# A decoder on one core: how the first layer's preparation waits, and what TensorE does meanwhile

## The reference

```python
mixed_qkv = hidden_states @ W_qkv                  # 128 -> 2048 channels
z = (hidden_states @ W_z).reshape(b_, t_, HV, DV)
beta = jax.nn.sigmoid(hidden_states @ W_b)
g = -jnp.exp(A_log) * jax.nn.softplus(hidden_states @ W_a + dt_bias)
mixed_qkv = _causal_conv_silu(mixed_qkv, conv_w)   # 4 taps along the tokens, then silu
q, k, v = jnp.split(mixed_qkv, [K_DIM, 2 * K_DIM], axis=-1)
...
q = _l2norm(q) * DK ** (-0.5)                      # _l2norm: x * rsqrt(sum(x * x) + EPS) per head
k = _l2norm(k)
```

## Time and profile before

| | us |
|---|---|
| median of 3 runs (lowest, highest) | 4723.59 (4719.43, 4734.4) |
| the profiled execution's own time | 4747.6 |
| its span, first to last instruction | 4745.9 |
| mean granted TensorE clock | 0.921 |

### The profile page before, as it was taken

The page is one execution under the profiler, slowest core; times in us unless marked ns, Lnnn a source line. Parts: engine busy times, 40 slices in busy tenths (PEclk is TensorE's granted clock), DMA queues, the critical chain, the costliest instruction groups (busy, mean ns, idle before and its releaser), DMA issues. The chain is left out here.

```text
span 4745.9 us, 96485 instructions
## 1 busy us (share of the span) xinstructions
PE 4029.2 (85%) x38268; PEld 2457.0 (52%) x38268; DVE 2463.7 (52%) x6106; ACT 1541.4 (32%) x3476; POOL 822.1 (17%) x1452
## 2 busy tenths in 40 slices
PE   6998787898799878789879977878887997787888
PEld 3883343465488334346548833434654883343465
DVE  4674534454567453445456744335545674434553
ACT  3452222341345222234134422223413442222431
POOL 1430000130153000013014300011301430001120
PEclk7998999999799899999979998999997998899999
DMA  2001000000000100000000010000000001000000
GB/s 80 3 3 43 15 18 18 22 36 25 25 3 3 51 7 18 18 22 36 25 25 3 3 57 1 18 18 22 35 25 25 3 8 52 8 11 18 23 35 27
DMA packets 11005, 105.56 MB, mean 22 GB/s; under 512 B 1148, under 2 KB 5552, under 8 KB 6192
## 3 DMA queue, kind: packets, MB, share of 16 engines
q1 hardware_dynamic: 10544, 99.21, 5.4%
HBM read 98.16 MB, written 1.05 MB: 21 GB/s over the span
## 5 line engine op out<-in xcount | busy, mean ns | idle before, releaser
L88 PE MATMUL psum<-ident_bf 128*128 128x512 bf16 x1784 | 515.5, 428 | 204.2 <-DVE l_attn_peak L770 66.6
L88 PEld LDWEIGHTS psum<-ident_bf 128*128 128x128 bf16 x1784 | 178.2, 108 | 465.3 <-issue 172.9
L3044 DVE TENSOR_TENSOR l_attn_xx<-l_attn_xx,psum 128x256 f32<-128x256 f32 x512 | 204.6, 419 | 207.4 <-PE psum L2649 195.6
L2811 ACT ACTIVATE l_attn_ax<-psum 128x128 f32<-128x128 f32 (+1 forms) x768 | 184.9, 279 | 366.1 <-PE psum L2630 251.4
L399 DVE TENSOR_TENSOR l_ffn_hidden<-l_ffn_silu,psum 128x512 f32<-128x512 f32 (+2 forms) x184 | 126.3, 686 | 325.3 <-ACT l_ffn_silu L340 325.1
L94 PEld LDWEIGHTS psum<-streamed_weights,l_ffn_hidden 128*128 128x128 f32 (+2 forms) x1728 | 226.0, 192 | 113.3 <-issue 99.8
L340 ACT ACTIVATE l_ffn_silu<-psum 128x512 f32<-128x512 f32 (+2 forms) x216 | 128.9, 597 | 475.9 <-PE psum L310 475.9
L2645 PE MATMUL psum<-l_attn_ax,l_attn_xx 64*64 64x64 f32 x5120 | 265.0, 222 | 0.0
L2649 PE MATMUL psum<-l_attn_xx,l_attn_ax 64*64 64x64 f32 x5120 | 258.2, 219 | 0.0
L770 DVE TENSOR_REDUCE l_attn_peak<-psum 128x4 f32<-128x2048 f32 (+3 forms) x128 | 185.9, 1487 | 126.2 <-PE psum L688 125.4
L2938 POOL TENSOR_TENSOR l_attn_part<-l_attn_ab,streamed_weights 128x128 f32<-128x128 f32 x640 | 243.3, 413 | 20.3 <-PE psum L2630 20.3
(11 more groups left out here) (522 smaller groups left out, 8141.6 us busy)
## 6 DMA issues: line engine op xcount, KB each, us to landing
streamed_weights<-pack_l_ffn SPq DMA_DIRECT2D x4, 5412.0 KB, 15.4
streamed_weights<-pack_l_ffn SPq DMA_DIRECT2D x4, 3972.0 KB, 13.3
streamed_weights<-pack_l_attn SPq DMA_DIRECT2D x5, 2848.5 KB, 9.4
streamed_weights<-pack_l_xattn SPq DMA_DIRECT2D x4, 2496.0 KB, 8.7
streamed_weights<-pack_l_ffn SPq DMA_DIRECT2D x4, 2192.0 KB, 8.0
streamed_weights<-pack_l_xattn SPq DMA_DIRECT2D x4, 2048.0 KB, 7.4
streamed_weights<-pack_l_ffn SPq DMA_DIRECT2D x4, 1923.0 KB, 8.0
streamed_weights<-pack_l_attn SPq DMA_DIRECT2D x4, 1107.5 KB, 4.9
```

The lines of the kernel that those rows point to most:

```text
L88: pe.matmul(self.bank(bank), self.ident_bf[:, :], self.ident_bf[:, :].unsqueeze(1).to_broadcast([P, NT, P]), start=True, stop=True)
L2811: act.activation(ax[b, p, :, :], m.psum[b, p, 0:P].rearrange("p (i t) -> p i t", i=2), ACT.Copy).then_inc(ax_ready, 1)
L3044: dve.tensor_tensor(both, both, m.psum[:, p, P:384], ALU.subtract).then_inc(x_less, 1)
```

## The change

Six edits, all in the preparation:

- `rsT` has 128 partitions; GpSimd clears it at the start of the block (a new semaphore, `rsT_cleared`), and ScalarE still writes 16 of them. The matrix of `spread` gets zeros in its other 112 rows, and its product runs over 128 rows. The packed array keeps its size.
- TensorE gets 8 identity products ahead of its wait for the roots at n = 11, and 6 ahead of the wait in front of projection 12.
- ScalarE's exp and logarithm go from n = 1 to n = 11, ahead of the copy of the turned roots, and VectorE's three instructions for g from n = 2 to n = 13.

```diff
-        rsT = psb("rsT", [HV, T])
+        rsT = psb("rsT", [P, T])
...
                     if n >= 2:
-                        if n <= NEWTON:
-                            m.warm(pe, 4, 7)
+                        if n <= NEWTON + 2 and n != NEWTON + 1:
+                            m.warm(pe, 4 if n <= NEWTON else 6, 7)
                         pe.wait_ge(conv_ready, n - 1)
...
                     if n == NEWTON + 1:
+                        m.warm(pe, 8, 7)
                         pe.wait_ge(rs_ready, 1)
...
-                    if n == 1:
+                    if n == NEWTON + 1:
                         act.activation(a_exp[:, :], w["a_log"], ACT.Exp)
                         act.activation(g_log[:, :, :], g_log[:, :, :], ACT.Ln).then_inc(logged, 1)
-                    if n == NEWTON + 1:
                         act.wait_ge(rs_turned, 1)
-                        act.activation(rsT[:, :], m.psum[0:HV, 6, :], ACT.Copy).then_inc(rsT_ready, 1)
+                        act.wait_ge(rsT_cleared, 1)
+                        act.activation(rsT[0:HV, :], m.psum[0:HV, 6, :], ACT.Copy).then_inc(rsT_ready, 1)
...
+                pool.memset(rsT[:, :], 0.0).then_inc(rsT_cleared, 1)
                 for i in range(2 * F):
...
-                    if n == 2:
+                    if n == NEWTON + 3:
                         dve.wait_ge(logged, 1)
...
-            ... ("spread", const["spread16"])]
+            ... ("spread", np.concatenate([const["spread16"], np.zeros((P - 16, 8, P), np.float32)]))]
```

More of the change, by code:

```diff
@@ L2266, in stage_l0_attn @@
         rsT_ready = sem("rsT")
+        rsT_cleared = sem("rsT_cleared")
         rs_spread = sem("rs_spread")
@@ L3494, in pack_l0_attn @@
             ("norm_w", np.tile(g("norm_w"), 2)[:, None]), ("out", tiles_of(g("W_out"))),
-            ("levels", np.concatenate([const["levels"][:64, :6, :64]] * 2)), ("ident_blocks", np.tile(np.eye(64, dtype=np.float32), (2, 1))), ("spread", const["spread16"])]
+            ("levels", np.concatenate([const["levels"][:64, :6, :64]] * 2)), ("ident_blocks", np.tile(np.eye(64, dtype=np.float32), (2, 1))), ("spread", np.concatenate([const["spread16"], np.zeros((P - 16, 8, P), np.float32)]))]
 OWN = ("levels", "spread8", "spread16", "forward", "inverse", "kernel_re", "kernel_re2", "kernel_im")
```

## The result

| | before | after |
|---|---|---|
| median (lowest, highest), 4 runs each | 4728.99 (4719.43, 4741.14) | 4679.61 (4675.36, 4684.64) |
| the profiled execution | 4747.6 | 4681.71 |
| its span | 4745.9 | 4680.1 |
| mean granted clock | 0.921 | 0.936 |

The ratio is 0.9887 with an interval of [0.9874, 0.9901]: 1.1% faster, 47 to 60 us, where 58 were forecast and the time was to be 4666.

What follows compares the result with a forecast made beforehand. TensorE, nearly always busy at a low clock, was taken to bound the block. Gains of 19 us in pass 1, 13.8 each in passes 2 and 4 and 11.2 in pass 3 made 57.8: 4723.6 to 4666 us, range 4643 to 4694.

Steps and rivals of the forecast that it cites:

- The bound: Whole block: TensorE nearly always busy at a mean clock of 0.68 to 0.74, so the clock bounds it.
- The chain: Projection 11 to the last copy, counted step by step at full clock: 27.0 us against 39.05.
- The tables' wait: Block's start: without exp and logarithm, silu starts 2.8 us earlier; a sure 2.8 us a pass.
- pass 1: Block's start in the first pass: the shortened wait ends before the clock falls, so it stays up, worth 8.0 us.
- Rival 4: Both clock falls, behind projection 2 and at the roots, are gone in all passes: 4646 us; chance 0.13.
- What holds the clock: Roots and spreads: products over 128 rows hold the clock; identity products fill 1.7 of the 1.85 us wait.
- Extra rows priced at nothing: Spreads: 128 rows stream the same 512 columns, so the extra rows cost nothing.
- The tail: Block's end: TensorE waits 1.8 us for v5 ahead of k0; 1 us a pass allowed for a low clock.
- Drains: Range of the total: a little more on both sides for drains and the 15 us run-to-run spread, 4643 to 4694.
- Rival 2: Block's last third: turns don't count as work, so the clock is down; 3 us more a pass, 4678; chance 0.10.
- The memset: GpSimd from the block's start: clearing 128x512 takes between nothing and 1.04 us, hidden, taken as zero.
- The time: Whole kernel: the median of 4723.6 less 57.8 us from the four blocks gives 4666 us.

Runs made afterwards that it cites:

- rows alone: The kernel before with only the 128-row spreads (zero rows) and the clearing of `rsT`: 4711.49 us, 0.9951 of before.
- fills at both ends: The changed kernel plus 6 and 3 identity products around projection 2, and 6 and 8 ahead of turns v6 and k0: 4666.30 us, 0.9853 of before.
- products alone: The kernel before with only the 8 and 6 identity products at the roots: 4702.71 us, 0.9932 of before.
- 64 rows: The kernel with fills at both ends, its spreads over 64 rows (48 of zeros) instead of 128: 4675.02 us, 0.9880 of before.

## Why the prediction was right, point by point

- **The bound.** Clock, not work: right. VectorE's 44 us stayed, and the clock in the section is 1.00 in three passes of four. The chain forecast 27.0 us to the end of the last copy, and 26.9 were measured (27.2 in the tables above, which go on to the next table load). The chain's points hold: silu of chunk 10 ended at 7.4 us behind projection 11 (forecast 7.3), turn v2 began at 8.0 (7.35 forecast: it also waits for a copy of v that stands behind silu on ScalarE, 0.6 that the chain left out).
- **The tables' wait.** 2.8 us of it were forecast and seen (3.46 to 0.66). The worth in a pass, 2.8, measured 3.0 to 3.2 in passes 2 to 4. The term that was mis-sized is pass 1: I let the clock stay up there for 8.0 us, since before it had fallen more than 4 us into the wait. It fell at about 38.3, in the wait of 0.66 behind projection 2, and the head gained 4.3. The prediction didn't look at how that pass began. Its trace has the clock at 0.50 ahead of the wait:

```profile
34.00:36.00 2.00, 2.00 (x4) 0.54 (x3) 0.73 (x1) 0.69 (x1) 0.00 (x0) 0.50 0.00 0
```

  In the kernel with the rows alone, pass 1 had the same low stretch, and its fall came as late. In the change the clock is 1.00 from 32 to 38 us and the fall came 7.3 us into the block, much as in the other passes. So the late fall went with a low stretch at the start, which also goes with a head 1.3 us longer than that of pass 2; why it comes stays open. Of the 4.3 us gained, about 3 are the tables' and the rest is chance. Rival 4, both falls gone in all passes, leant on the same late fall, and no pass of the change showed it; its price, blocks of 55.8 us, is what the fills at both ends measured, 55.76.
- **What holds the clock.** I credited the zero rows and only let the products "hide in waits". In the sections products alone gave 39.5 us and rows alone 42.2, so either would have done most of it; the total was right because they overlap.
- **Extra rows priced at nothing.** At the same clock, loads of weights stood exposed behind the 16 and the 64 rows (the idle 0.76 us) and not behind the 128 (0.24): turn k0 came 0.4 us sooner with 128 rows in a kernel without fills in the tail, and with them the section was 1.45 us shorter. The sign stood in the earlier trace rows, 1.12 us for a spread at full clock against 1.02 for a projection that follows at once.
- **The tail.** 1 us a pass was allowed for a low clock; it cost 1.2 in one pass of four.
- **Drains.** The range of the forecast has something in it for drains behind the table loads. No run shows the term. Behind the roots' copy, as ScalarE's rows after show, the load runs 1.28 and silu starts 0.02 us behind its end:

```profile
1237.61 1.28 ACT L2381 ACT_TABLE_LOAD   x1
1238.91 0.63 ACT L2381 ACTIVATE l_attn_vT<-l_attn_conv 128x512 f32<-128x512 f32 x1
```

  Before, the three loads and two activations at the head took 4.37 us, which is 3 x 1.28 and 0.5 for the activations. The wait of 1.23 us ahead of turn v2 is no sign of a drain: 0.6 of it is the copy of v.
- **Rival 2, turns don't count,** falls too. It was a supposition of mine, with no row for it. In three passes of the change the clock is 1.00 through the tail, and in the kernel with fills at both ends it is 1.00 through a tail of six turns, two spreads and 14 identity products, so the clock didn't fall with this many turns; what turns alone would do isn't shown.
- **The memset** is 0.52 us of GpSimd in its idle time, and nobody waits.
- **The time.** 57.8 us were forecast; the blocks gave 56.9, the profiled executions differ by 65.9 and the medians by 49.4. Two misses in the sum cancel: the heads gave 13.7 us where 16.4 were forecast (pass 1), the sections 43.1 where 41.4 were, as the tail fell in one pass and not in all. So the mechanism was right and the closeness of the total, 1 us, is partly luck. The time came out 14 us above 4666: the medians gave 8 us less than the forecast gain, and a fourth run moved the median of before up by 5.

## What to carry to other kernels

Ask of each wait of TensorE what the granted clock does behind it, and price a wait by the steps at the low clock that follow: in the kernel before, 10 to 34 us of low clock behind 2 to 4 us of waiting. Two cures for one fall don't add (here 42.2 and 39.5 us in the sections, each alone); take each back alone before crediting it. A fill that hides in a wait today stands in the way once something ahead of it gets slower, as the 8 identity products ahead of turn k0 did with 64 rows, by 0.8 us. Where the effect is a few blocks' clock and the rest of the program wanders by 35 us, compare the blocks.

## What the runs showed of the hardware

- With 16 and with 64 rows in the spreads, both loads of weights of the projection behind two spreads began with the projection itself, 0.76 us after the load before them had ended; with 128 rows the first began 0.43 us ahead of the projection, 0.24 us after the load before it. With fills in the tail and the clock at 1.00 the section took 28.65 us (16 rows) and 28.7 (64) against 27.2. Without fills there TensorE had 1.73 to 1.93 us to spare ahead of turn k0, and k0 started 22.80 us behind projection 11 with 16 rows and 22.42 with 128.
- With products alone the clock stayed at 1.00 over the loop's six spreads of 16 rows and fell only in the unfilled tail (sections of 28.4, the fall among them). With fills at head and tail and a wait of 1.23 us left ahead of the spreads, 16 rows lost it in one section of four, 64 and 128 rows in none; that is one profile of each.
- Unchanged code took 4421 to 4456 us in fourteen profiles, and the same head 33.5 to 38.3 us, depending on when the clock fell and came back. What makes the clock come back stays open; no run isolates it.
